# LoRA's output product moved into the next step, with norm 2 scaled by VectorE

## The reference, cut to what matters

```python
x = x + tanh(g_xattn[0]) * L0_xattn(layernorm(x), ctx)   # 32 heads of 128, 8 kv heads, q and k rms-normed
x = x + tanh(g_ffn[0])   * L0_ffn(layernorm(x))          # LoRA with a router over 8 experts of rank 16
x = x + tanh(g_xattn[1]) * L1_xattn(layernorm(x), ctx)   # 16 heads of 96, 4 kv heads
x = x + tanh(g_ffn[1])   * L1_ffn(layernorm(x))          # silu(gate) * up, then down; 1792 wide
# L0_ffn:
scores = 8 * softmax(x @ Wr.T + br)
out = 2 * einsum('bshr,hor,bsh->bso', x @ A, B, scores)
```

## Time and profile before

| | before |
|---|---|
| median of 3 runs | 1188.02 us |
| profiled execution | 1189.01 us |
| its span | 1187.2 us |
| PE busy | 1129.7 us, 95% |
| DVE busy | 844.7 us, 71% |
| ACT busy | 836.9 us, 70% |
| POOL busy | 374.2 us, 32% |
| granted TensorE clock, mean | 0.99 |

### The profile page before, as it was taken

One profiled execution on the slowest core, in us unless ns is written; L12 is line 12 of the kernel. 1 busy time (PEld: TensorE's weight loads), 2 busy tenths in 40 slices (PEclk: granted clock), 3 DMA queues, 4 the chain that ended last, 5 costly groups with the idle time before them and its releaser, 6 DMA issues.

```text
span 1187.2 us, 22719 instructions
## 1 busy us (share of the span) xinstructions
PE 1129.7 (95%) x7184; PEld 712.0 (60%) x7184; DVE 844.7 (71%) x2050; ACT 836.9 (70%) x2711; POOL 374.2 (32%) x685
## 2 busy tenths in 40 slices
PE   6789999999999999999999978799999999799998
PEld 4445666666666666666666645566676766455554
DVE  5578767767767767777677678988888888743434
ACT  5678878888888888878888677777777665522221
POOL 5554434334733333333343354321111121000000
PEclk9899999999999999999999999999999999999999
DMA  6465554464655545555545646758996796200000
GB/s 242 105 143 120 130 130 103 120 139 89 133 144 128 118 99 130 125 112 129 122 98 112 135 93 135 146 132 173 229 193 142 139 166 126 52 1 1 36 1 36
DMA packets 411991, 139.55 MB, mean 118 GB/s; under 512 B 386656, under 2 KB 396640, under 8 KB 411872
## 3 DMA queue, kind: packets, MB, share of 16 engines
q1 hardware_dynamic: 409968, 134.43, 51.2%
q0 software_dynamic: 1904, 3.67, 1.1%
HBM read 39.21 MB, written 2.10 MB: 35 GB/s over the span
## 4 chain that ended last, share of the span: by engine, by line
PE 79%; DVE 9%; ACT 5%; issue 3%; POOL 2%; DMA 1%; DVEq 0%; POOLq 0%; ACTq 0%
PE bank L519 22%; PE bank L520 22%; PE bank L521 22%; PE bank L720 8%; PE bank L739 4%; ACT probs L906 2%; DVE pieces L1084 2%; DVE stats L1095 1%; DVE mx L1185 1%; DVE x L1222 1%; ACT junk L811 1%; POOL rstd L1473 1%; DVE q_rows L1084 0%; DVE nb L1195 0%; DVE nb L1190 0%
## 5 line engine op out<-in xcount | busy, mean ns | idle before, releaser
L808 ACT ACTIVATE pieces<-probs,rs 128x256 f16<-128x256 f32 x384 | 166.3, 524 | 10.2 <-DVE rs L1202 9.4
L1185 DVE TENSOR_REDUCE mx<-bank 128x2 f32<-128x512 f32 x192 | 131.5, 685 | 56.8 <-PE bank L521 56.7
L1084 DVE SCALAR_TENSOR_TENSOR pieces<-probs,rs,pieces 128x256 f16<-128x256 f32 x384 | 163.3, 485 | 5.8 <-ACT pieces L808 5.0
L906 ACT ACTIVATE probs<-bank,nb,rq 128x256 f32<-128x256 f32 x256 | 141.1, 564 | 37.2 <-DVE nb L1190 36.9
L519 PE MATMUL bank<-wq,xT 128*128 128x512 f16 (+1 forms) x384 | 139.1, 362 | 2.7 <-DVE wq L1084 2.7
L519 PE MATMUL bank<-wo_hi,oT 128*128 128x512 f16 x352 | 133.4, 379 | 6.0 <-DVE oT L1084 4.6
L520 PE MATMUL bank<-wq,xT 128*128 128x512 f16 (+1 forms) x384 | 138.9, 362 | 0.0
L521 PE MATMUL bank<-wq,xT 128*128 128x512 f16 (+1 forms) x384 | 138.7, 361 | 0.0
L811 ACT ACTIVATE junk<-bank 128x128 bf16<-128x128 f32 x384 | 101.7, 289 | 52.0 <-PE bank L521 51.8
L521 PE MATMUL bank<-wo_hi,oT 128*128 128x512 f16 x352 | 133.4, 379 | 0.0
L520 PE MATMUL bank<-wo_lo,oT 128*128 128x512 f16 x352 | 133.4, 379 | 0.0
(11 more groups left out here) (187 smaller groups left out, 2651.2 us busy)
## 6 DMA issues: line engine op xcount, KB each, us to landing
raw_o<-in_wo_a SPq DMA_DIRECT2D x8, 1024.0 KB, 5.8
raw_q<-in_wq_a SPq DMA_DIRECT2D x7, 1024.0 KB, 5.9
raw_kv<-in_wkv_a SPq DMA_DIRECT2D x8, 512.0 KB, 3.8
turned<-pieces SPq DMA_TRANSPOSE x192, 2.8
raw_q<-in_wq_c SPq DMA_DIRECT2D x4, 768.0 KB, 5.0
raw_o<-in_wo_c SPq DMA_DIRECT2D x4, 768.0 KB, 5.1
down_rest<-in_down_t POOLq DMA_DIRECT2D x5, 512.0 KB, 4.3
ff_in<-in_gate_t SPq DMA_DIRECT2D x4, 448.0 KB, 4.0
```

The source lines that it names most:

```text
L808: return act.activation(out, in_, ACT.Copy, scale=scale)
L906: act.activation(probs[:, h, :], bank[h // 2][:, (h % 2) * KV:(h % 2 + 1) * KV], ACT.Exp, bias=nb[:, h:h + 1], scale=scale, accum_out=sums ...
L1084: return dve.scalar_tensor_tensor(out, in_, scale, hi, ALU.mult, ALU.subtract)
L1185: dve.tensor_reduce(mx[:, pr], chunks(bank[i][:, :], 2), AX.X, ALU.max, negate=True).then_inc(mx_done, 1)
```

## The change

Five edits. (1) `lora_project_out` of a tile moves from the end of a PE step to the next step, behind the k and v projections (`kv_proj`), and its result goes to bank 3 instead of bank 2; PE's wait for `lora_add` ahead of `lora_project` falls, and the product itself waits for the `lora_add` before it. (2) `lora_add` and `norm_stats(2, t)` move from the end of DVE's step to the start of the next. (3) In steps 59 to 66 the low pieces of weights move from the end of DVE's step to the start of the next. (4) Norm 2 is scaled on DVE once (`norm_scale(2, t)`, behind the first row maximum) instead of on ACT twice; POOL makes the high piece with a copy, no longer computes a shift for it, and does `norm_rstd(2)` behind the rows of norm 1. (5) The scaling of the row maxima becomes a plain `tensor_tensor` in layer 0 and a `tensor_scalar` in layer 1, and the tile `zeros` goes.

```diff
+        def low_late(n):
+            return beside(n + 1)[3] is not None
...
             def lora_project_out(t):
                 pe.wait_ge(lora_lo, t + 1)
-                mm3(bank[2][:, :], tT[t % 2], lb, start=True, stop=True).then_inc(lora_out, 1)
+                if t >= 1:
+                    pe.wait_ge(lora_added, t)
+                mm3(bank[3][:, :], tT[t % 2], lb, start=True, stop=True).then_inc(lora_out, 1)
...
                 if T < N:
                     kv_proj(T)
-                if lora is not None and lora >= 1:
-                    pe.wait_ge(lora_added, lora)
-                if n == N0 + 3:
-                    pe.wait_ge(lora_added, NT)
+                if norm2 is not None:
+                    lora_project_out(norm2)
...
                 values(n)
-                if lora is not None:
-                    lora_project_out(lora)
...
-                if norm2 is not None:
-                    norm_scaled(2, norm2)
...
-                    dve.scalar_tensor_tensor(nb[:, pr], mx[:, pr], 1.0, rq[:, c:c + 2], ALU.mult, ALU.mult
-                                             ).then_inc(nb_done, 1)
+                    dve.tensor_tensor(nb[:, pr], mx[:, pr], rq[:, c:c + 2], ALU.mult).then_inc(nb_done, 1)
...
-                    dve.scalar_tensor_tensor(nb[:, pr], mx[:, pr], es[:, g % 2, s:s + 1], zeros[:, :], ALU.mult, ALU.add
-                                             ).then_inc(nb_done, 1)
+                    dve.tensor_scalar(nb[:, pr], mx[:, pr], es[:, g % 2, s:s + 1], None, ALU.mult).then_inc(nb_done, 1)
...
                 if n >= 1:
                     o_low(n - 1)
+                if n >= 1 and low_late(n - 1):
+                    for chunk in weight_chunks(n - 1):
+                        weight_low(*chunk)
+                if norm2 is not None:
+                    lora_add(norm2)
+                    norm_stats(2, norm2)
...
                 if S < N:
                     row_max(S, 0)
+                if norm2 is not None:
+                    norm_scale(2, norm2)
...
-                for chunk in weight_chunks(n):
-                    weight_low(*chunk)
-                if lora is not None:
-                    lora_add(lora)
-                    norm_stats(2, lora)
+                if not low_late(n):
+                    for chunk in weight_chunks(n):
+                        weight_low(*chunk)
...
-                if k in (1, 2):
+                if k == 1:
                     pool.wait_ge(norm[k].rstd, t + 1)
...
-                if k == 0:
+                if k in (0, 2):
                     pool.tensor_copy(rows[:, 0:D], xn[xn_slot(k, t)]).then_inc(norm[k].row_hi, 1)
...
                 if norm1 is not None:
                     norm_rstd(1, norm1)
-                if norm2 is not None:
-                    norm_rstd(2, norm2)
...
                 if norm2 is not None:
+                    norm_rstd(2, norm2)
                     norm_rows(2, norm2)
```

More of the change, by code:

```diff
@@ L207, in build @@
         half_neg = sb("half_neg", NT)
-        zeros = sb("zeros", 2)
         half_pos = sb("half_pos", NT)
@@ L1100, in norm_scale @@
                 dve.wait_ge(norm[k].rstd, t + 1)
+                if k == 2 and t >= 1:
+                    dve.wait_ge(norm[k].row_lo, t)
                 if k in (0, 3) and t >= 2 and turned_by_dma(k, t - 2):
@@ L1252, in lora_add @@
                 dve.wait_ge(lora_out, t + 1)
-                dve.scalar_tensor_tensor(xt[:, t, :], bank[2][:, :], tg_lora[:, 1:2], xt[:, t, :],
+                dve.scalar_tensor_tensor(xt[:, t, :], bank[3][:, :], tg_lora[:, 1:2], xt[:, t, :],
                                          ALU.mult, ALU.add).then_inc(lora_added, 1)
@@ L1670, in _ @@
             pool.memset(both_half[:, 1:2], 0.5).then_inc(consts, 1)
-            pool.memset(zeros[:, :], 0.0).then_inc(consts, 1)
             pool.memset(kb[:, :], XS * XS * RMS_EPS * L0.hd).then_inc(consts, 1)
@@ L1674, in _ @@
             norm_rstd(0, 1)
-            pool.wait_ge(consts, 9)
+            pool.wait_ge(consts, 8)
             kv_scale(0)
```

## The result

| | before | after |
|---|---|---|
| median of 6 runs each | 1188.14 us (1186.46 to 1189.14) | 1193.14 us (1192.18 to 1195.39) |
| profiled execution, its span | 1189.01, 1187.2 us | 1194.91, 1192.9 us |

The ratio is 1.0044 with a 95% interval of [1.0033, 1.0055]: slower by 5.0 us. The forecast was 1190.5, slower. The two profiled executions differ by 5.9, since that of after lies 1.8 above its median and that of before 0.9.

What follows compares the result with a forecast made beforehand. It took DVE, not PE, to bound steps 61 to 64, with PE binding again behind step 67. Terms +2.8, +1.5, -1.8, -0.3 and +0.3 summed to +2.5 us: 1190.5 us, own range 1188.5 to 1192.5, wide range 1183 to 1195.5.

Steps and rivals of the forecast that it cites:

- PE's 14 us: PE's waits on `tT_lo` (11.7 us) and `lora_add` (2.5 us), claimed to come back at DVE's next product.
- a new wait for POOL's power: DVE ahead of `norm_scale(2)`, steps 61 to 65: stands 1.3 us in each, from 4.0 to 5.3 behind the mark.
- steps 61 to 64: Distances between DVE's marks behind norm 1's statistics: 13.6 us each, 54.4 against 51.6, +2.8.
- Step 65: The step without a norm 1 for the next: 12.0 us against 10.5, +1.5.
- step 66: The step without norm 1, POOL free: 11.1 us against 12.9, -1.8.
- PE's late product: In step 66, DVE's 1.44 us wait for it goes; with the time at the low clock, a gain of 1.8 us.
- step 67: From step 66's end to PE's last norm 2 transfer: 9.6 us against 9.88, -0.3.
- step 60: DVE no longer waits 0.8 us for PE but stands 1.5 for POOL's power: +0.3.
- the rest: From PE's last norm 2 transfer to the span's end: as before.
- A: Rival, chance 0.30: POOL's power is there when DVE comes, wait under 0.2 us; -3.5 us, 1184.5.
- B: Rival, chance 0.15: PE falls to the low clock waiting for norm 2's rows; +4 us more, 1194.5.
- C: Rival, chance 0.15: it evens out, DVE's gaps being smaller than counted; 0, 1188 us.

Runs made afterwards that it cites:

- e10: The kernel before plus two unused DVE copies behind the first `nb` in steps 61 to 65: 1189.27 us, ratio 1.0004.
- e12: The changed kernel plus two unused DVE copies right ahead of `norm_scale(2)` in steps 61 to 65: 1193.42 us, ratio 1.0042.
- e6: The changed kernel without edit 3, so the weights' low pieces stay at the end of DVE's step: 1195.57 us, ratio 1.0058.
- e2: The kernel before with edit 1 alone (LoRA's output product behind the next k and v projections, in bank 3): 1187.92 us, ratio 0.9999.
- e5: The kernel before with edit 4 alone, POOL's power for norm 2 kept where it was: 1189.80 us, ratio 1.0011.
- e1: The kernel before with edit 5 alone (row maxima scaled by `tensor_tensor` and `tensor_scalar`): 1188.40 us, ratio 0.9998.
- e3: The changed kernel with edit 4 undone (norm 2 scaled twice on ACT, POOL's power ahead of norm 1's rows): 1191.31 us, ratio 1.0022.
- e4: The changed kernel with POOL's power for norm 2 put back ahead of norm 1's subtraction: 1192.62 us, ratio 1.0036.
- e9: The kernel before with edit 1 and the row maxima of units 60 to 68 scaled as two single columns: 1192.08 us, ratio 1.0024.
- e11: The changed kernel with `norm_scale(2)` behind the second `nb` instead of the first: 1195.28 us, ratio 1.0057.
- e8: The kernel before with the row maxima of units 60 to 68 scaled by two single-column `tensor_scalar`: 1188.78 us, ratio 1.0002.

## Why the prediction was right, and where it was not

**The mechanism.** The prediction said that PE's 14 us would not be won, that a new wait for POOL's power would come up in front of `norm_scale(2)`, and that `nb` would go on being held. The first two are in the trace; the third only in part, as told below. In steps 61 to 64 the forecast was 13.6 each and they took 13.7 on average (14.26, 13.44, 13.90, 13.35: the prediction worked out one step and used it for all four). In step 62 its parts fit too: ACT starts at 1.48 (I took 1.5), the scaling at 5.28 (5.3), the second `nb` ends at 7.7 (7.9), and from there to the next mark it is 5.7 (5.7). Step 65 was 11.85 for 12.0. The wait itself is 0.94 for 1.3, since DVE arrives 4.3 behind the mark and not 4.0. The second `nb` was to stand for 0.6 us and takes 0.27: it starts later because POOL's copy holds `lora_scale`'s `lg` (0.60 us instead of 0.23), a hold that the prediction didn't count, and it ends with the subtraction all the same. All holds of `nb` together fell from 6.1 to 2.1 us. That it is the chain through POOL which sets the pace, and not DVE's work, was in the sum (each step was worked out along that chain), but the text's first reason was the other: "PE waits because DVE has more to do". e10 and e12 contradict that sentence, and e6 shows the chain's side: 0.32 later at its head, 0.33 longer step.

**The mis-sized term: step 66.** Forecast 11.1, measured 12.34; of the -1.8 only -0.6 came. The prediction let POOL and PE be on time there. But in step 65 PE stands idle for 3.94 us, for `lora_act` now, and the granted clock is 0.63 in the 3.4 us behind, where it was 0.51 before; its product comes late as before, and DVE waits 0.39 for `oT` and 0.63 for the product, 1.02 together. e2 had shown the same with edit 1 alone: the wait moves, from 1.44 to 1.54. The -1.8 named as "PE's late product" was the term without a row that excluded its return. Where the clock does stay high there, as in e5, step 66 takes 10.98 us and most of the term comes.

**The sum.** The forecast missed where its range was narrow: 1193.14 lies outside the forecast's own 1188.5 to 1192.5 and inside the wide range only. Against the sum, steps 61 to 65 took 0.4 more, step 66 1.2 more, step 67 0.5 less and step 60 0.4 less (-0.1 for +0.3, from `y_add` of unit 58 to the mark of step 61). In part these cancel: PE got its last tile 3.3 us later for 2.5, and that it is so near is in part luck. (The rows give 3.49 us for the transfer that the sum took as 3.45.) The larger miss is the rest.

**PE's waits.** I expected about 2 us for `xT<-n_rows` in each step. They were 0.67 to 1.50, five times, and the large ones stood at `lora_act` (11.2 us), which I had not listed as a place where the lateness could show, although it is queued behind the same wait on DVE.

**The rest.** I had it as unchanged, and in the profiled execution it took 2.1 to 2.4 us more. Nothing that runs there was changed but the form of `nb`, and e1 shows that form to be free. In after PE's waits at `values`, at the first product with turned pieces, add to 2.0 us between 795 and 966 us (one of 0.89 put down to the transfer, the others to "issue") against 0.75 before; the granted clock is 1.00 there. e12, whose program behind 795 us is after's, has a rest of 395.6 in its profile (the fastest of its five executions), so the edits do not force this; e10, which only shifts the stage's end by 2.2 us, leaves the rest at 395.6 as well, so a shift alone doesn't either. The medians exceed before's by more than the stage explains in after, e3, e4, e5, e6, e9 and e11 (1.5 to 2.7 us more), and not in the others (1.1 less to 0). In e9 the low clock behind the wait for norm 2's last rows gives most of it. In after no such stretch is there; what the transfers meet was not isolated, and this part of the cause stays open. By the traces the stage accounts for 3.5 us of the loss.

**The rivals.** A needed a wait under 0.2 us; it was 0.94. e4 made it 0 and the time stayed 4 us over before's, so A's price for it (6 us) was wrong as well: the standing goes to `nb`. B's place (PE falling to the low clock on norm 2's transfers) is not in after's trace, since its longest wait there is 1.5 us. But what B feared came at another wait: I counted no low clock behind 2.25 us, and behind 2.22 us for `lora_act` in step 61 the granted clock is 0.60 for 3.3 us. From the second `nb`'s end to the next mark that step takes 6.05 us and steps 62 to 64 5.69, so it cost about 0.4 us (an estimate from these numbers). The experiments show B's own place: 0.50 to 0.54 behind waits for norm 2's rows of 2.47 us (e2), 3.32 (e9) and 4.31 (e11), and 0.51 behind 1.66 (e3), yet 1.00 behind 2.01 (e3). C's smaller gaps did not come.

**What each edit is worth.** Alone, edit 5 is 0 (e1), edit 1 is 0 (e2), edit 4 costs 0.11% [0.01%, 0.21%] (e5). Edits 1, 2, 3 and 5 together cost 0.22% (e3), all five 0.44%, without edit 3 0.58% (e6). In the stage edit 4 wins 0.9 us alone, by the high clock in step 66, and loses 2.5 with edits 1 to 3 in place and POOL's power last. DVE's wait for the power comes from POOL's order: with the power ahead of the subtraction it is 0 with edits 1 to 3 (e4) and without them (e5). Edits 1 to 3 make the statistics of norm 2 ready 2.9 us behind the mark in step 62 instead of 2.3, and between e5 and e4 (which has edits 1 to 3 and 5 besides) steps 61 to 65 grow by 0.7 us and step 66 by 1.8, with the granted clock at 0.58 there in e4. How the loss divides between the later statistics and the clock was not isolated. No version tried beats the kernel before.

## What to carry to other kernels

A busy share of 94% does not make an engine the one that sets the pace: if some of its instructions stand until another engine's end, work put ahead of them costs little (3.3 us added cost 1.35 and 0.7 us of the stage), and taking holds away won nothing here. Adding a known piece of unused work tells this in one run, and was the clearest of these experiments. Look at the granted clock of the same stretch before comparing two kernels: a stretch of low clock that one of them escapes was worth 1.3 us here, more than most of the edits. Before moving work a half step later, follow the chain through every engine that waits for it, and look for the same lateness at each point queued behind the new wait, not only at the wait that was removed.

## What the runs showed of the hardware

- A `tensor_tensor` of 128x2 on DVE is held until the end of a POOL subtraction of 128x512 (0.87 us, e1), as is a `tensor_scalar` of 128x2 (0.88), 128x4 (1.12, e11) and 128x8 (1.03, e10). A `tensor_scalar` of 128x1 is not (0.34 for two, e8).
- The granted clock behind a wait of PE was 0.50 to 0.63 for some 3 us after 1.66 (e3), 2.22 (after), 2.47 (e2), 3.23 (before), 3.94 (after) and 4.31 us (e11), and 1.00 after 2.01 (e3) and 2.66 us (e5). The length of the one wait ahead does not tell it.
- POOL's copy of 128x512 took 0.61 us in the stage, and a `tensor_scalar` of 128x8 beside it 0.60 instead of 0.23.
- The hold works the other way too: POOL's `var_e` of 128x1 takes 0.59 us beside DVE's `wo_lo` (e6) and 0.19 beside its `oT`, which reads a bank.
- A copy of 128x512 from float32 to the float32r type by `tensor_scalar` with a constant took 0.33 us from start to start (e10), where the same operation with two scale operands from memory and float32 output takes 0.46 (726.14 to 726.60 in after).
